# A recurrent front and sparse attention on one core: lags as float32 matmuls on 32-row tiles, a new order of the group step, and a later close of the last group

## What is computed

```python
# layer 0, a gated bank of decaying traces
ctx    = causal_ema(x, tau_ctx)
gated  = x * sigmoid([x, ctx] @ Wg.T + bg)
h1     = gelu(x @ Wn1.T + bn1)
mod    = 0.5 + sigmoid(h1 @ Wn2.T + bn2)              # 32 numbers a position
traces = [causal_ema(gated * mod[..., d], tau_raws[d]) for d in range(32)]
temporal = sum_d traces[d] * softmax(blend, axis=0)[d]
gate   = sigmoid(temporal @ Wtemp.T + btemp)
soma   = gelu(x @ Wsoma.T + bsoma)
x      = x + layernorm((soma * gate) @ Wout.T) * gamma + beta
# layer 1, attention, 16 heads of 8 channels, 32 listed neighbours a query or all keys
q, k, v = x @ Wq.T + bq, x @ Wk.T + bk, x @ Wv.T + bv
x      = x + (softmax(q k / sqrt(8) + bias of the row) v) @ Wo.T + bo
```

## Time and profile before

| what | value |
|---|---|
| timed runs | 328.13, 328.15, 328.81 us; median 328.15 |
| profiled execution | time 326.89 us, span 325.0 us, granted TensorE clock 0.999 |
| TensorE busy | 306.1 us (94%), weight loads 207.0 (64%) |
| VectorE busy | 274.6 us (85%) |
| GpSimd busy | 248.8 us (77%) |
| ScalarE busy | 215.2 us (66%) |
| DMA | 23.07 MB, 71 GB/s mean |

### The profile page before, as it was taken

The page is one execution under the profiler, slowest core; times in us unless marked ns, Lnnn a source line. Parts: engine busy times, 40 slices in busy tenths (PEclk is TensorE's granted clock), DMA queues, the critical chain, the costliest instruction groups (busy, mean ns, idle before and its releaser), DMA issues. The chain is left out here.

```text
span 325.0 us, 9974 instructions
## 1 busy us (share of the span) xinstructions
PE 306.1 (94%) x3314; PEld 207.0 (64%) x3324; DVE 274.6 (85%) x1449; ACT 215.2 (66%) x459; POOL 248.8 (77%) x300
## 2 busy tenths in 40 slices
PE   8898899999999999999887989999999999999995
PEld 2554464656566465555535667887887887887873
DVE  3888899878978886797879669999999999999972
ACT  5862256545655655457674678878778878778863
POOL 3173586778686885665855869999999999999990
PEclk9999999999999999999999999999999999999999
DMA  6700120050311305013530435564544364210011
GB/s 184 222 2 1 32 67 34 17 130 3 105 42 57 90 0 144 4 33 65 75 60 2 87 95 83 82 139 126 126 105 117 93 126 105 78 32 6 3 34 34
DMA packets 29154, 23.07 MB, mean 71 GB/s; under 512 B 2736, under 2 KB 27824, under 8 KB 29104
## 3 DMA queue, kind: packets, MB, share of 16 engines
q1 hardware_dynamic: 29104, 22.44, 29.3%
HBM read 7.75 MB, written 2.10 MB: 30 GB/s over the span
## 5 line engine op out<-in xcount | busy, mean ns | idle before, releaser
L1609 POOL TENSOR_TENSOR arena<-arena,neg_max 128x512 f32<-128x512 f32 x128 | 129.9, 1052 | 10.8 <-DVE neg_max L1451 10.7
L1451 DVE CUSTOM_DVE_ANT_0 arena<-ps,arena 128x128 f32<-128x128 f32 x512 | 113.9, 287 | 9.6 <-issue 5.1
L1093 ACT ACTIVATE arena<-ps 128x512 f32<-128x512 f32 x128 | 69.6, 596 | 10.2 <-PE ps L789 10.2
L789 PE MATMUL ps<-ident_sb,arena 128*128 128x128 f32 x512 | 68.2, 276 | 0.0
L789 PEld LDWEIGHTS ps<-ident_sb,arena 128*128 128x128 f32 x512 | 56.5, 141 | 6.9 <-POOL arena L1609 4.0
L1528 POOL TENSOR_TENSOR arena<-arena 128x448 f32<-128x448 f32 (+6 forms) x56 | 42.8, 764 | 23.2 <-DVE arena L1283 19.6
L1451 DVE DVE_READ_ACCUMULATOR2_ANT neg_max<- 128x1 f32 x512 | 42.6, 83 | 0.0
L805 PE MATMUL ps<-arena 128*32 128x128 f32 x1024 | 41.2, 279 | 0.0
L1515 POOL TENSOR_TENSOR arena<-decay_a,arena 128x192 f32<-128x192 f32 x32 | 19.5, 637 | 22.0 <-ACT arena L930 22.0
L805 PEld LDWEIGHTS ps<-arena 128*32 128x32 f32 x1024 | 24.1, 109 | 6.9 <-issue 0.3
L775 PE MATMUL ps<-arena 48*128 48x128 bf16 x512 | 25.4, 219 | 2.4 <-DVE neg_max L1451 2.3
(11 more groups left out here) (172 smaller groups left out, 575.4 us busy)
## 6 DMA issues: line engine op xcount, KB each, us to landing
arena<-q_parts SPq DMA_DIRECT2D x96, 64.0 KB
arena<-k_parts SPq DMA_DIRECT2D x96, 64.0 KB
arena<-in_x SPq DMA_DIRECT2D x16, 256.0 KB, 3.3
arena<-in_xt SPq DMA_DIRECT2D x8, 256.0 KB, 2.8
out<-arena SPq DMA_DIRECT2D x7, 256.0 KB, 3.0
arena<-in_consts SPq DMA_DIRECT2D x1, 420.0 KB, 3.8
w_sb<-in_w SPq DMA_DIRECT2D x1, 384.0 KB, 6.3
w_sb<-in_w SPq DMA_DIRECT2D x1, 192.0 KB, 4.1
```

The lines of the kernel that those rows point to most:

```text
L789: mm = pe.transpose(ps[1][:, q % 2, k * P:k * P + P], neg_t[q % NT_RING][:, k * P:k * P + P], ident)
L1093: act.activation(probT[q % PT_RING], ps[1][:, q % 2, :], ACT.Exp, scale=-1.0)\
L1451: dve.tensor_tensor_reduce(out=neg_t[q % NT_RING][:, cs], in0=ps[0][:, score_bank(c) + slot, cs], in1=nbias[n % 2], scale=1.0, scalar=3.0e ...
L1609: pool.tensor_tensor(t4, t4, neg_max[:, n % 2, 4 * z:4 * z + 4].unsqueeze(2).broadcast_to([P, 4, P]), ALU.subtract).then_inc(s["shifted"], 1)
```

## The change

It does the following.

- **Lags.** `f_lags` on TensorE is replaced by `four_lags`: one float32 matmul a lag, over the 32 rows of one copy (lag k uses copy k mod 4), so that four consecutive ones lie in four row groups; with w_lag as weights, no longer scaled by a quarter. They go to four banks (`lag_bank`). lag_a, lag_b, mod_pa, mod_pb, `lag_parts`, `f_mod_part1`, `f_mod_part1b` and `f_mod_parts` are gone. The products get buffers of their own.
- **Banks.** The context of a group lies in bank 3 instead of 1, c_v in bank 3 instead of 2, and the gate (`gate_bank`) in bank 0, b_cross's, instead of 2, but for the last group.
- **Order of a step.** Rewritten on TensorE, ScalarE, VectorE and GpSimd (in the diff); f_hidden moves one step ahead (group m + 2 in step m); c_less and c_v come last. The first step has an order of its own, with one added matmul of 384 columns into a bank that is not read. ScalarE's logarithm of the counts moves behind c_values.
- **Passage to attention.** logits(5) comes before b_mixed, logits(6) and (7) before c_moments, logits(8) to (11) before c_residual(LAST, 1); scores(3) before b_out; bias_sum(2) in GpSimd's `end`; the close of group 7 runs two octets later (c = 4 to 8), behind scores of its octet, and SOLO is 12 instead of 10.

```diff
-SOLO = 10
+SOLO = 12
...
+        def ctx_bank(i, m):
+            return bank(1, 1) if at_start(i, m, 2) else bank(m % 2, 3)
+        def lag_bank(m, lag):
+            return bank(m % 2, lag % 2) if lag in (0, 1, 6, 7) else bank(1 - m % 2, 2 + lag % 2)
+        def gate_bank(i, m):
+            return bank(m % 2, 2 if last_group(i, m) else 0)
...
@@ TensorE
+            def four_lags(i, m, first):
+                u = m % 2
+                if first == 0:
+                    pe.wait_ge(s["soma_ready"], grp(i, m, 1, 1))
+                    pe.wait_ge(s["modn_ready"], grp(i, m, 1, 1))
...
+                        pe.wait_ge(s["bh_ready"], grp(i, m, NJ + NCAR))
+                else:
+                    pe.wait_ge(s["prod_ready"], grp(i, m, Q, 4))
+                for lag in range(first, first + 4):
+                    rows_of = slice((lag - first) * D, (lag - first) * D + D)
+                    pe.matmul(lag_bank(m, lag), w_lag[rows_of, lag, :], thd[u][rows_of, :], start=True, stop=True)\
+                        .then_inc(s["lag_ps"], 1)
...
             def f_hidden(i, m):
-                    pe.wait_ge(s["mixed_ready"], grp(i, m, 1, -1))
+                    pe.wait_ge(s["prod_ready"], grp(i, m, Q, 5 - Q))
             def f_context(i, m):
+                    pe.wait_ge(s["centred"], grp(i, m, GB, -GB))
             def b_out(i, m):
                 pe.wait_ge(s["mixed_ready"], grp(i, m, 1, 1))
+                if not last_group(i, m):
+                    pe.wait_ge(s["prod_ready"], grp(i, m, Q, Q + 6))
...
+            def step(i, m):
+                f_modulation(i, m + 1)
+                b_carries(i, m)
+                f_gate_x(i, m + 1)
+                f_context(i, m + 1)
+                b_locals(i, m)
+                f_soma(i, m + 1)
+                f_modulation_n(i, m + 1)
+                f_gate_ctx(i, m + 1)
+                c_x1T(i, m - 1)
+                four_lags(i, m + 1, 0)
+                f_gated(i, m + 1)
+                b_cross(i, m)
+                c_k(i, m - 1)
+                b_crossT(i, m)
+                four_lags(i, m + 1, 4)
+                c_less(i, m - 1, 1, 0)
+                b_gate(i, m)
+                c_less(i, m - 1, 1, 1)
+                c_q(i, m - 1)
+                if not last_group(i, m + 1):
+                    f_hidden(i, m + 2)
+                b_out(i, m)
+                c_less(i, m - 1, 0, 0)
+                c_v(i, m - 1)
+                c_less(i, m - 1, 0, 1)
...
@@ TensorE, first step
+                b_locals(i, m)
+                f_modulation_n(i, m + 1)
+                f_gate_ctx(i, m + 1)
+                value_bias()
+                b_cross(i, m)
+                four_lags(i, m + 1, 0)
+                b_crossT(i, m)
+                f_gated(i, m + 1)
+                b_gate(i, m)
+                four_lags(i, m + 1, 4)
+                pe.wait_ge(s["gn_ready"], 2)
+                pe.matmul(bank(1, 2)[:, 0:W_FIRST * P], wt["wg_x"], w_sb[:, 0:W_FIRST, :].rearrange("p k c -> p (k c)"),
+                          start=True, stop=True)
+                b_out(i, m)
+                f_hidden(i, m + 2)
...
@@ ScalarE, step
+                f_modulation(i, m + 1)
+                f_context(i, m + 1)
+                f_soma(i, m + 1)
+                f_modulation_n(i, m + 1)
+                f_gate(i, m + 1)
+                c_x1T(i, m - 1)
+                f_gated(i, m + 1)
+                b_cross(i, m)
+                c_part(i, m - 1, 1, 0)
+                c_part(i, m - 1, 1, 1)
+                b_gate(i, m)
+                c_part(i, m - 1, 1, 2)
+                c_part(i, m - 1, 0, 0)
+                if not last_group(i, m + 1):
+                    f_hidden(i, m + 2)
+                c_part(i, m - 1, 0, 1)
+                c_values(i, m - 1)
                 if i * 2 + m == COUNTED:
                     act.wait_ge(s["vec_step"], vec("cnt_none"))
                     act.activation(lncnt[:], cnt1[:], ACT.Ln).then_inc(s["lncnt_ready"], 1)
+                c_part(i, m - 1, 0, 2)
...
@@ VectorE, step
+                b_carries(i, m)
+                if at_start(i, m, 2):
+                    key_tables()
+                b_locals(i, m)
+                f_gated(i, m + 1)
+                f_lags(i, m + 1, range(0, 4))
+                b_temporal(i, m)
+                f_lags(i, m + 1, range(4, 6))
+                if first < last:
+                    counts(first)
+                if 2 * i + m == COUNTED:
+                    late_tables()
+                b_mixed(i, m)
+                f_lags(i, m + 1, range(6, Q))
+                if first < last:
+                    counts(first + 1)
+                c_moments(i, m)
+                c_centre(i, m)
...
@@ VectorE, end
                 b_temporal(LAST, 1)
                 logits(4)
+                logits(5)
                 b_mixed(LAST, 1)
-                logits(5)
-                c_moments(LAST, 1)
                 logits(6)
                 logits(7)
+                c_moments(LAST, 1)
                 c_centre(LAST, 1)
...
@@ VectorE, octet_step
-                if c == 1:
-                    c_residual(LAST, 1)
                 if 1 <= c and c + 3 < 2 * B:
                     logits(2 * c + 6)
                     logits(2 * c + 7)
+                if c == 2:
+                    c_residual(LAST, 1)
...
@@ TensorE, octet_step
-                if c == 2:
-                    c_x1T(LAST, 1)
...
                 if 1 <= c and c + 3 < 2 * B:
                     scores(c + 3)
+                if c == 4:
+                    c_x1T(LAST, 1)
+                if c == 5:
+                    c_qk(LAST, 1)
+                if c == 6:
+                    c_less_both(LAST, 1, 0)
+                if c == 7:
+                    c_less_both(LAST, 1, 1)
+                if c == 8:
+                    c_v(LAST, 1)
```

310 lines of the change are left out of this document (90 added, 220 removed).

## The result

The changed kernel takes 324.83 us (median of 4 runs, 324.03 to 325.73) against 328.48 for the kernel before on the same chip (4 runs, 328.13 to 329.01): ratio 0.9888, 95% interval 0.9857 to 0.992. It is faster, by 3.65 us and not by 13, and above the range that was given. The kernel before takes about 326.6 in some executions and 328.1 or more in others, its profiled one (326.89) was of the first kind and its four here of the second, and so the medians lie 3.65 apart and the profiled executions 2.22.

The account below looks back on a forecast made before the run. TensorE's own work was taken to bound the front; gains of 8.3 (steps), 4.0 (head) and 0.7 us (entry) sum to 13.0, so 328.15 becomes 315.2 us. The range was 310.5 to 321.0.

Parts of the forecast that it names:

- the last b_out: Last front step: late_tables ahead of b_mixed on VectorE makes b_out 0.75 us late, the step 18.4 us.
- T0: Start of scores(0), where the entry into attention begins; 155.34 us before, forecast at 143.05.
- scores(5): Entry: reordered logits remove its 1.03 us idle for VectorE; moves from T0 + 24.05 to T0 + 22.5.
- the steps: Six front steps up to scores(0): 107.65 us instead of 115.92, a gain of 8.3 us.
- the head: Start up to the first full step: 35.4 us instead of 39.42, a gain of 4.0 us, between 2 and 5.
- the entry: From scores(0) to scores(12): 43.85 us instead of 44.55, net 0.7 us gained, between -2 and +3.5.
- the 0.25 allowed in each of four steps for `counts`: Front: the second `counts` makes c_centre late, so four steps take 17.9 us instead of 17.65.
- the rival with the right size for a step: Front: VectorE ends last more often at hand-overs; steps 18.6 to 19.0 us, 319 to 322 in all; chance 0.20.
- normalise and result between them 2.25: Entry: time for these two, added to the octets, in the sum that put scores(12) at T0 + 43.85.
- Seven of these are 16.45: Entry: seven octets on one bank pair, each a chain of scores and eight logits of 2.35 us.
- The Ln's 1.5: Entry: Ln behind c_values delays bias_terms, x1 and c_x1T; 1.5 us lost, or 0 if c_centre is not late.
- The entry rival: Entry: added single-bank octets and late x1 cost what reordering gives; 317 to 319 us; chance 0.12.

Follow-up runs that it names:

- e7: Changed kernel with every four lags issued twice, the first result written over; 337.72 us, ratio 1.0288.
- e6: Changed kernel with the turned modulation (f_modulation_n) ahead of f_soma in every step; 322.61 us, ratio 0.9852.
- i1: Changed kernel, but GpSimd waits for c_residual(LAST, 1) to be done before it goes on; 323.6 us, ratio 0.9899.
- e4: Changed kernel with ScalarE's Ln of the counts ahead of q's second piece and c_values; 322.43 us, ratio 0.9853.

## Why the prediction was wrong in size

**The sign and the bottleneck were right.** TensorE's own work bounds the front, the lags run side by side, a wait of 0.5 appears ahead of b_locals, the last b_out is late by 0.99 (0.75 was said), the Ln makes c_x1T late (T0 + 6.13, said 6.3), and scores(5) comes at T0 + 22.35 (said 22.5). Of 13.0 us, 3.65 came between the medians and 2.2 between the profiled executions: 4.4 are missing in the steps, 1.3 in the head and 5.1 in the entry.

**The steps: 3.9 us gained, 8.3 said.** The sum took each instruction's start-to-start time from its old neighbours. The price of another form was named in it and then set to nothing by a misreading: it says that b_locals takes 0.95 "between two 128-row instructions", but in the earlier trace rows the instruction behind b_locals, at 103.75, has 32 rows. With 128 rows on both sides it takes 1.06 in the changed kernel. The new order puts 32-row instructions next to 128-row ones in more places: b_locals and soma 1.06 and 1.05 for 0.95 and 0.86, the four lags 1.19 and 1.07 for 0.99, x1T and crossT 0.53 for 0.44. These six and the wait that is 0.1 longer than said come to 0.9 a step, 18.53 and not 17.65; 0.12 of it is the wait for VectorE ahead of f_gated. Over the six steps 4.4 are missing and not 5.3, because the 0.25 allowed in each of four steps for `counts` came to 0.12 at most. e7 and e6 show it for the lags and for b_locals; for the others it is read from the traces. The lags were one term of it, 0.28 us a step with that wait and 0.16 without. The estimate from the Trainium skill, "TensorE: Matmul & The Clock Gate", Part 3, of 1.12 for four lags is 0.05 above the 1.07 that the trace shows between other forms, nearer than the prediction's 0.99. The text had the rival with the right size for a step (18.6 to 19.0, a gain of 4 to 6 less) but with a wrong cause, hand-overs to VectorE: VectorE is busy 14.50 of 18.52 and ends the 0.51 ahead of b_locals and the 0.12, no more.

**The head: 2.7 us gained, 4.0 said.** b_locals started at 23.46 and not 22.7, because VectorE's last product of the carries (L1263), for which it waits 0.50, ended at 23.32 and not 22.6; and the first step, from there on, took 13.26 where 12.7 was assumed. What made either longer was not tried.

**The entry: 4.4 us lost, 0.7 gain said.** Three steps of it failed. (1) c_residual was set to 1.4 from a row in which GpSimd was in its way for 0.48 us only; it took 2.98, as GpSimd had then four shifts, a bias_sum and two more shifts without a break (i1). (2) "normalise and result between them 2.25" was counted as work, but they stand behind c_residual and c_keep, and TensorE behind them: 2.42 idle, then 0.92 for ScalarE (L1092; 0.65 in the kernel before). (3) "Seven of these are 16.45": the added octets were priced at 2.35 each, where the close (x1T, k, q, three bf16 pieces, v) now falls into a stretch in which TensorE is the bound; the octets from scores(7) on took 4.27, 4.46, 2.68, 3.98 and 3.23, with 1.7 us of idle time in these 18.6. The Ln's 1.5 was right (1.3 to 1.6 by e4) and is in the total. The entry rival (0.12) was right in kind and put at 317 to 319, 2 to 4 us above the forecast for what was 5.1.

**The range** ended at 321.0 because no case joined the two rivals. Each alone would have been held (319.6 and 320.3); nothing ties one to the other, so the case of both should have been priced as well: 324.7 without the head, 326.0 with it. That the measured 324.83 is so near the first is chance: the forecast started from the median of before, 1.26 above its profiled execution, and the changed kernel's median is 0.16 above its own.

## What to carry to other kernels

A duration from a trace belongs to its neighbours. On TensorE count a change of tile form at each end; on VectorE ask whether both inputs are in SBUF and whether GpSimd is at work then, and look at the shortest and the longest of a group, not at its mean; the kernel before showed the sign already (L1260 at 0.81 and at 1.75). When work is moved out of a stretch where another engine is behind into one where TensorE is the bound, it costs its whole length there; and before a good reordering is given up, look for one collision in it, as a single added wait turned a version from 321.7 into 317.8 us.
